# A gated cross-attention layer: new prologue with fp32 row-tiled weight folds, maxima by PE transpose, and double-buffered scores and x

## The chip, the cores and the metric

The kernel runs on one core of one Trainium2 chip. The metric is device time in microseconds (us); the time given is the median over runs. Engines: TensorE (PE), VectorE (DVE), ScalarE (ACT), GpSimd (POOL), and SyncE (SP), which here only issues DMA.

## The reference

```
h   = x + tanh(g_xattn) * (attention(layernorm(x), ctx) @ Wo + bo)
out = h + tanh(g_ffn)   * (layernorm(h) @ W[idx] + b[idx])
attention: q = ln(x) @ Wq, k = ctx @ Wk, v = ctx @ Wv, 16 heads of 64,
           softmax(q k^T / 8) v
idx = argmax(log_softmax(logits) + gumbel(u))       (one of 8 matrices)
```

x is (4, 2048, 512), ctx (4, 77, 384), Wq (512, 1024), Wk and Wv (384, 1024), Wo (1024, 512), W (8, 512, 512), all fp32.

## The kernel before

There are only 77 keys a batch, so the kernel folds the weights once. Prologue: for each batch A = Wq k^T (512 x 16*77) and VW = v Wo (16*77 x 512). Loop: 64 tiles of 128 rows of x, batch by batch in turn, each with scores = ln(x) A, softmax, out = P VW, layer norm and one matrix of the feed-forward.

fp32 precision is kept with fp16 matmuls: an operand is held as high and low fp16 halves and a product is three matmuls (`split_products`, L1014 to 1019). The halves need a power of two as scale, from the largest absolute value over the whole matrix: VectorE takes maxima along the row (`part`, `half`), GpSimd's `partition_all_reduce` (`share`, L453) the maximum over partitions, `power_of_two_scale` (L723) makes the scale.

For the folds (`fold`, L1058) the values and keys are laid out as block diagonals of head pairs (`v_diag`, `k_diag`), so that one 128-row matmul serves two heads: per pair and 128 columns of weights ("a unit") six matmuls of 308 columns. There are 4 slots of 8 units for the values and as many for the keys. ScalarE writes a unit's high half (L619, L643), VectorE the low half (`low`, L290; called at L827 and L841). The folded values are written transposed into `slots`, and 16 DMA transposes (L361, four a slot, on SyncE's queue) bring them into `vw`. `a_split` (the folded keys) lies over the slots, so the key fold waits for transposes (L640, L838).

Before the loop, SyncE then loads the biases and waits for all transposes. The loop is a software pipeline: step n of PE does scores(n), attention(n-1), ffn(n-2) (L1155). VectorE does the softmax of tile n (`maxima`, `shift`, `softmax`, `probs_low`), the layer norm of x tile n+1 (`x_moments` to `x_low`) and the rest of n-1 to n-3. SyncE transposes x (L334), probabilities (L415 to 422) and the second layer norm (L390) by DMA. Scores have three PSUM banks, and the scores of tile n wait for `shifted` of tile n-1 (L1103); x transposed has one buffer (L332). GpSimd computes reciprocal square roots and residual sums. In step (0, 0) VectorE also takes the maxima of the feed-forward matrix, and GpSimd its `share(WF)` (L533); its halves are written in the first steps (L678, L868).

## Time and profile before

| | us |
|---|---|
| median of 3 runs (1121.66 to 1122.82) | 1122.08 |
| the profiled execution: span from first to last instruction | 1116.9 |
| PE busy | 1067.9 (96%) |
| VectorE busy | 964.6 (86%) |
| ScalarE busy | 361.4 (32%) |
| GpSimd busy | 301.4 (27%) |

The span is that of one profiled execution; the times of runs are taken without a profile and include what lies around the span. The mean granted TensorE clock is 0.983 of full. In the rows, a block of a timeline is merged from neighbouring instructions, its name is that of the first, and "xN" counts them. "big", "vw_arena", "banks" are the names of the memory areas; `banks` is PSUM. Lines of helpers (L290 `low`, L1018 `split_products`) stand for all their callers.

### The profile page before, as it was taken

Reading aid. Unit: us, or ns where it says so; the run is one execution under the profiler, and the core shown is the slowest. Engines: PE = TensorE matmul, PEld = TensorE weight load, DVE = VectorE, ACT = ScalarE, POOL = GpSimd, SP = SyncE. Lnnn points to the kernel's source line nnn. Section 1 sums busy time; section 2 is a strip of 40 time slices with the busy share of each in tenths; the row PEclk is TensorE's granted clock in tenths of the full one; section 3 lists DMA queues with packets and bytes.
Section 4 is the critical chain, followed back from the end, with each engine's and each line's share of the span. In section 5 each row is a group of like instructions: output and inputs, shape, how many; then the busy total and the mean of one; then the engine's idle time right before and its main releaser. Section 6 shows DMA issues by size and latency. Waiting matters only on the chain.

```text
span 1116.9 us, 16454 instructions
## 1 busy us (share of the span) xinstructions
PE 1067.9 (96%) x5452; PEld 546.1 (49%) x5452; DVE 964.6 (86%) x1423; ACT 361.4 (32%) x562; POOL 301.4 (27%) x416
## 2 busy tenths in 40 slices
PE   7687879999999999999999999999999999999997
PEld 5455534444454444454544445544445554444542
DVE  6676869999888899888899988889988888998884
ACT  3586432233232223223223323222332322232331
POOL 4361222122222222222222222222222222222221
PEclk9889889999999999999999999999999999999999
DMA  9069625545545544554554554554455455455543
GB/s 327 10 111 200 153 56 113 109 105 121 114 108 116 122 101 111 122 107 109 122 112 104 117 117 108 113 122 104 107 122 111 108 119 114 105 114 115 112 98 76
DMA packets 365720, 129.49 MB, mean 116 GB/s; under 512 B 345039, under 2 KB 345347, under 8 KB 365699
## 3 DMA queue, kind: packets, MB, share of 16 engines
q1 hardware_dynamic: 365635, 129.22, 53.1%
q8 instruction: 12, 0.20, 0.1%
q14 instruction: 9, 0.07, 0.0%
q0 software_dynamic: 64, 0.00, 0.0%
HBM read 26.43 MB, written 16.78 MB: 39 GB/s over the span
## 4 chain that ended last, share of the span: by engine, by line
PE 83%; DVE 6%; ACT 3%; DMA 2%; issue 2%; SPq 2%; POOL 1%; POOLq 0%; DVEq 0%; ACTq 0%
PE banks L1018 81%; PE banks L1137 2%; DVE big L290 2%; SPq L361 2%; DMA big<-big 1%; ACT big L619 1%; DVE big L768 1%; DVE stats L745 1%; DMA xT_area<-big 1%; POOL vw_arena L465 0%; DMA vw_arena<-big 0%; DVE big L892 0%; ACT vw_arena L562 0%; DMA big<-in_ctx 0%; DVE stats L901 0%
## 5 line engine op out<-in xcount | busy, mean ns | idle before, releaser
L1018 PE MATMUL banks<-big,xT_area 128*128 128x462 f16 (+1 forms) x2316 | 418.1, 339 | 11.9 <-DMA xT_area<-big 11.9
L1018 PE MATMUL banks<-vw_arena,big 128*128 128x512 f16 (+1 forms) x1920 | 414.1, 373 | 14.1 <-DVE big L290 8.9
L1018 PEld LDWEIGHTS banks<-big,xT_area 128*128 128x128 f16 x2316 | 226.2, 98 | 204.2 <-DMA xT_area<-big 13.6
L1018 PEld LDWEIGHTS banks<-vw_arena,big 128*128 128x128 f16 (+1 forms) x1920 | 188.3, 99 | 219.3 <-issue 8.7
L1018 PE MATMUL banks<-big 128*128 128x512 f16 (+1 forms) x948 | 203.4, 367 | 10.3 <-DVE big L290 7.2
L524 POOL TENSOR_TENSOR stats<-stats,cst 128x1 f32<-128x1 f32 x64 | 12.3, 192 | 658.2 <-DVE stats L948 658.2
L290 DVE SCALAR_TENSOR_TENSOR big<-big 128x512 f16<-128x512 f32 (+1 forms) x194 | 180.9, 933 | 3.5 <-ACT big L655 1.4
L886 DVE TENSOR_REDUCE stats<-banks 128x6 f32<-128x462 f32 (+1 forms) x192 | 111.7, 582 | 79.0 <-PE banks L1018 78.9
L1018 PEld LDWEIGHTS banks<-big 128*128 128x128 f16 (+1 forms) x948 | 93.3, 99 | 110.5 <-issue 12.5
L700 ACT ACTIVATE big<-big 128x1232 f16<-128x1232 f32 (+1 forms) x66 | 79.2, 1199 | 207.5 <-DVE big L905 207.3
L655 ACT ACTIVATE big<-big 128x512 f16<-128x512 f32 x64 | 40.3, 630 | 326.5 <-DVE big L966 326.5
L686 ACT ACTIVATE big<-big,cst 128x462 f32<-128x462 f32 (+1 forms) x192 | 120.6, 628 | 59.2 <-DVE big L892 59.2
L892 DVE TENSOR_TENSOR big<-banks,stats 128x462 f32<-128x462 f32 (+1 forms) x192 | 111.7, 582 | 2.3
L768 DVE TENSOR_SCALAR big<-big,stats 128x512 f32<-128x512 f32 x64 | 97.8, 1527 | 8.5 <-POOL stats L447 8.5
L905 DVE TENSOR_TENSOR big<-big,cst 128x1232 f32<-128x1232 f32 (+1 forms) x66 | 92.6, 1403 | 2.3
L901 DVE TENSOR_REDUCE stats<-big 128x16 f32<-128x1232 f32 (+1 forms) x66 | 92.2, 1396 | 1.3
L502 POOL TENSOR_TENSOR big<-big 128x512 f32<-128x512 f32 x64 | 83.1, 1300 | 0.1
L537 POOL TENSOR_TENSOR big<-big 128x512 f32<-128x512 f32 x64 | 81.4, 1273 | 3.5 <-DVE big L966 3.5
L571 ACT ACTIVATE big<-big 128x512 f16<-128x512 f32 x64 | 40.3, 630 | 106.4 <-DVE big L768 106.4
L290 DVE SCALAR_TENSOR_TENSOR big<-banks,big 128x616 f32 (+2 forms) x72 | 48.8, 724 | 16.9 <-ACT big L643 11.0
L923 DVE SCALAR_TENSOR_TENSOR big<-banks,cst,big 128x512 f32<-128x512 f32 x64 | 47.7, 746 | 5.2 <-PE banks L1018 5.2
L932 DVE SCALAR_TENSOR_TENSOR big<-banks,cst,big 128x512 f32<-128x512 f32 x64 | 47.7, 745 | 4.6 <-PE banks L1137 4.5
(84 smaller groups left out, 544.9 us busy)
## 6 DMA issues: line engine op xcount, KB each, us to landing
big<-in_x SPq DMA_DIRECT2D x65, 256.0 KB, 2.7
out<-big SPq DMA_DIRECT2D x64, 256.0 KB, 2.2
big<-big SPq DMA_TRANSPOSE x133, 3.2
vw_arena<-in_L_xattn_Wq SPq DMA_DIRECT2D x2, 1024.0 KB, 12.8
vw_arena<-in_L_xattn_Wo SPq DMA_DIRECT2D x2, 1024.0 KB, 16.8
big<-in_L_xattn_Wv SPq DMA_DIRECT2D x2, 768.0 KB, 8.2
big<-in_L_xattn_Wk SPq DMA_DIRECT2D x2, 768.0 KB, 14.8
xT_area<-big SPq DMA_TRANSPOSE x65, 3.1
```

The costliest lines, as they stand in the source:

```text
L290: return nc.vector.scalar_tensor_tensor(out=lo, in0=value, scalar=scale, in1=hi, op0=ALU.mult, op1=ALU.subtract)
L502: nc.gpsimd.tensor_tensor(res[:, b1, :], xin[:, b1 % 2, :], bias[:, 0, :], ALU.add).then_inc(res_ready, 1)
L537: nc.gpsimd.tensor_tensor(res[:, b2, :], res[:, b2, :], bias[:, 1, :], ALU.add).then_inc(x2b_ready, 1)
L686: nc.scalar.activation(probs[:, cols], probs[:, cols], ACT.Exp, scale=exp_scale).then_inc(exp_done, 1)
L700: nc.scalar.activation(ps[:, h0 * J:h1 * J], probs[:, h0 * J:h1 * J], ACT.Copy, scale=2.0 ** PROB_BITS).then_inc(p_hi, 1)
L768: nc.vector.tensor_scalar(xn, xin[:, b1 % 2, :], mv1[:, 0:1], rstd1, ALU.subtract, ALU.mult).then_inc(xn_ready, 1)
L886: nc.vector.reduce_max(mx[:, h0:h1], by_head(s_ps[:, k, 0:(h1 - h0) * J]), AX.X).then_inc(mx_ready, 1)
L892: nc.vector.tensor_tensor(by_head(probs[:, h0 * J:h1 * J]), by_head(s_ps[:, k, 0:(h1 - h0) * J]), mx[:, h0:h1].unsqueeze(2).to_broadcast([ ...
L901: nc.vector.reduce_sum(sums[:, h0:h1], values, AX.X).then_inc(sum_ready, 1)
L905: nc.vector.tensor_tensor(values, values, factors.unsqueeze(2).to_broadcast([P, h1 - h0, J]), ALU.mult).then_inc(p_ready, 1)
L923: nc.vector.scalar_tensor_tensor(out=outb[:, b3 % 2, :], in0=f_ps, scalar=f_scale, in1=res[:, b3, :], op0=ALU.mult, op1=ALU.add).then_inc( ...
L1018: mm = nc.tensor.matmul(ps, lhs(l), rhs(r), start=first and n == 0, stop=last and n == 2)
```

## The change

- Folds: no block diagonals and no fp16 halves of the operands. A unit is two fp32 matmuls of 64 rows each (`unit`), head e = 0 on partitions 0 to 63 into one bank, e = 1 on partitions 64 to 127 into the next. Only the result is split into halves. vT (and wqT when it is copied out of PSUM) is multiplied by one product of scales. All 64 units are written out instead of partly looped. PE's value fold has three bank pairs, the key fold four.
- Key matmuls stand between the units of the value fold (`key_piece`). The queries' transposes come at its end.
- Maxima over partitions: a PE transpose of the column of maxima, spread over 128 columns, and a VectorE maximum along the row (`spread`, `power_of_two`). GpSimd's `partition_all_reduce` is gone everywhere.
- Load order: Wv, Wo, Wk, W[idx], Wq; x tiles 0 and 1 after the value fold, from ScalarE's queue. The feed-forward matrix is scaled and split in the prologue by GpSimd and ScalarE. Key maxima, Wq maxima and the x preparation of tiles 0 and 1 stand between the units on VectorE.
- Memory: raw weights and ctx lie where the transposed values (`vw`) go; `a_split` lies over the slots and the raw feed-forward matrix; the key fold of quarter k waits for the transposes of slot k. SyncE's order is slots 0 to 2, x tile 0, biases, slot 3, x tile 1.
- Loop: scores alternate between banks 0 to 2 and 5 to 7 and wait for `shifted` of tile n-2; x transposed has two buffers. The first scores wait for the whole key fold. Step (0, 0) no longer holds x and matrix work.

The core of the diff:

```diff
+        fold_area = sb("fold_area", [P, KT * SLOT_WORDS])
+        a_split = fold_area[:, 0:A_WORDS].bitcast(F16).rearrange("p (k s b n) -> p k s b n", s=2, k=KT, b=B)
+        slots = fold_area[:, :].bitcast(F16).rearrange("p (t b n) -> p t b n", t=KT, b=B)
...
+        vw_area = sb("vw_area", [P, KT * SLOT_WORDS])
+        vw = vw_area[:, :].bitcast(F16).rearrange("p (t b c n) -> p t b c n", t=KT, b=B, n=P)
...
-        s_ps = banks[:, 0:3, :]
+        s_ps = [banks[:, 0:3, :], banks[:, 5:8, :]]
...
+        V_BANKS = [0, 4, 2]
+        A_BANKS = [6, 2, 0, 4]
...
+        def pair_banks(first):
+            return banks[:, first:first + 2, 0:BJ].rearrange("p e (b j) -> p e b j", b=B)
...
+        def pair_of_heads(cols):
+            return cols.rearrange("p b (e j) -> p e b j", e=2)
...
-                if n == 0:
-                    sp.dma_start(xin[:, 0, :], x[0, 0:P, :]).then_inc(x_first, 16)
...
-                sp.dma_start(wq_raw[:, rows, :], wq.rearrange("(k p) n -> p k n", p=P)[:, rows, :]).then_inc(wq_loaded[n], 16)
...
             sp.wait_ge(idx_ready, 1)
...
             sp.dma_start(wf_raw, ffn_w[bass.ds(op, 1), :, :].rearrange("o (k p) n -> p (o k) n", p=P)).then_inc(wf_loaded, 16)
...
-                if positive(q1, b1, 1):
-                    due(s_done, nth(q1, b1, len(BANKS)))
-                sp.dma_start_transpose(xT.rearrange("p s k n -> p (s k) n"),
+                if positive(q1, b1, 2):
+                    due(s_done, nth(q1, b1, len(BANKS)) - len(BANKS))
+                sp.dma_start_transpose(xT[:, b1 % 2].rearrange("p s k n -> p (s k) n"),
...
+            for t in range(KT - 1):
+                turn_values(t)
+            turn_x(0, 0)
+            sp.wait_ge(vwT_done, 2 * UNITS)
             sp.dma_start(bias[:, 0, :], bo.rearrange("(a n) -> a n", a=1).to_broadcast([P, D])).then_inc(bias_loaded, 16)
...
+            turn_values(KT - 1)
+            turn_x(0, 1)
...
-            def share(k):
...
-                pool.wait_ge(amax_ready, k + 1)
-                nc.gpsimd.partition_all_reduce(amax_all[:, k:k + 1], amax[:, k:k + 1], P,
-                                               bass.bass_isa.ReduceOp.max).then_inc(amax_shared, 1)
...
+            pool.wait_ge(scale_f_ready, 1)
+            nc.gpsimd.tensor_tensor(wf_flat, wf_flat, scale_f.to_broadcast([P, KT * D]), ALU.mult).then_inc(wf_scaled, 1)
...
+            act.wait_ge(scale_v_ready, 1)
...
+            nc.scalar.activation(vT[:, 5:HP, :], vT[:, 5:HP, :], ACT.Copy, scale=scale_v).then_inc(v_scaled_end, 1)
...
+                act.wait_ge(vwT_done, 2 * (u + 1))
+                nc.scalar.copy(pair_of_heads(slots[:, t, :, h * PW:(h + 1) * PW]), pair_banks(V_BANKS[u % 3])).then_inc(vwT_hi, 1)
...
+                for h in range(HP):
+                    value_high(t, h)
+                act.wait_ge(vwT_hi, (t + 1) * HP)
+                nc.scalar.copy(slots[:, t, :, LOW + BODY:LOW + BODY + TAIL], slots[:, t, :, BODY:HJ]).then_inc(vwT_tail, 1)
...
+            for r in range(2):
+                act.dma_start(xin[:, r, :], x[r, 0:P, :]).then_inc(x_loaded[r], 16)
...
+            for h in range(0, HP, 2):
+                act.wait_ge(wqT_done, h + 1)
+                nc.scalar.activation(wqT[:, h, :], banks[:, WQ_BANKS[h], :], ACT.Copy, scale=scale_q).then_inc(wqT_even, 1)
...
+                    v = k * HP + h
+                    act.wait_ge(a_done, 2 * (v + 1))
+                    nc.scalar.copy(pair_of_heads(a_split[:, k, 0, :, h * PW:(h + 1) * PW]), pair_banks(A_BANKS[v % 4])).then_inc(a_hi, 1)
+                    if v == 5:
+                        x_high(0, 0)
+                    if v == 22:
+                        x_high(0, 1)
...
+            def power_of_two(m, bank):
...
+                dve.wait_ge(amax_spread[m], 1)
+                nc.vector.reduce_max(top[:, m:m + 1], banks[:, bank, 0:P], AX.X).then_inc(pow_step[m], 1)
+                dve.wait_ge(pow_step[m], 1)
+                nc.vector.tensor_scalar(pow2[:, m:m + 1].bitcast(U32), top[:, m:m + 1].bitcast(U32), 0x7F800000, None,
+                                        ALU.bitwise_and).then_inc(pow_step[m], 1)
+                dve.wait_ge(pow_step[m], 2)
+                nc.vector.reciprocal(rcp[:, m:m + 1], pow2[:, m:m + 1]).then_inc(pow_step[m], 1)
...
+            dve.wait_ge(floor_set, 1)
+            value_part(0)
...
+                dve.wait_ge(wo_loaded[n], 16)
+                part(WO, n, wo_raw[:, n * HP // 2:(n + 1) * HP // 2, :])
+            largest(WO)
+            value_part(1)
+            value_part(2)
+            value_part(3)
+            largest(VV)
+            power_of_two(WO, 4)
+            power_of_two(VV, 0)
...
+            nc.vector.scalar_tensor_tensor(out=scale_v, in0=rcp[:, VV:VV + 1], scalar=2.0 ** FOLD_BITS, in1=rcp[:, WO:WO + 1],
...
+            dve.wait_ge(scale_v_ready, 1)
+            for h0, h1 in ((0, 2), (2, 5)):
+                nc.vector.tensor_scalar(vT[:, h0:h1, :], vT[:, h0:h1, :], scale_v, None, ALU.mult).then_inc(v_scaled, 1)
...
+            dve.wait_ge(wf_loaded, 16)
+            part(WF, 0, wf_raw)
+            largest(WF)
...
+            def value_low(t, h):
...
+                first = V_BANKS[u % 3]
+                dve.wait_ge(vwT_hi, u + 1)
+                if h < HP - 1:
...
+                    nc.vector.tensor_tensor(pair_of_heads(slots[:, t, :, LOW + h * PW:LOW + (h + 1) * PW]), pair_banks(first),
+                                            pair_of_heads(slots[:, t, :, cols]), ALU.subtract).then_inc(vwT_lo, 1)
+                else:
+                    for e, start, stop, beyond in LAST_LOWS:
+                        key = (HEADS - 2 + e) * J
+                        nc.vector.tensor_tensor(slots[:, t, :, key + beyond + start:key + beyond + stop], one_bank(first, e, start, stop),
+                                                slots[:, t, :, key + start:key + stop], ALU.subtract).then_inc(vwT_lo, 1)
...
+                    value_low(t, h)
+                    if (t, h) == (0, 1):
+                        power_of_two(WF, 7)
+                        dve.wait_ge(pow_step[WF], 3)
+                        nc.vector.tensor_scalar(scale_f, rcp[:, WF:WF + 1], 2.0 ** WF_BITS, None, ALU.mult).then_inc(scale_f_ready, 1)
+                    if (t, h) == (0, 3):
+                        key_part(0)
+                    if (t, h) == (KT - 1, 3):
+                        power_of_two(KK, 6)
+                        power_of_two(WQ, 7)
...
+                        nc.vector.scalar_tensor_tensor(out=scale_q, in0=rcp[:, KK:KK + 1], scalar=2.0 ** FOLD_BITS, in1=rcp[:, WQ:WQ + 1],
...
+                    if t == 1 and h in (2, 5):
+                        n = h // 3
+                        dve.wait_ge(wq_loaded[n], 16)
+                        part(WQ, n, wq_raw[:, n * KT // 2:(n + 1) * KT // 2, :])
+                if t < KT - 1:
+                    key_part(t + 1)
+                if t == 1:
+                    largest(WQ)
+                if t == 2:
+                    largest(KK)
...
+                    dve.wait_ge(a_hi, v + 1)
+                    nc.vector.tensor_tensor(pair_of_heads(a_split[:, k, 1, :, cols]), pair_banks(A_BANKS[v % 4]),
+                                            pair_of_heads(a_split[:, k, 0, :, cols]), ALU.subtract).then_inc(a_lo, 1)
+                    if v == 1:
+                        x_moments(0, 0)
+                    if v == 2:
+                        dve.wait_ge(x_stats, 1)
+                        x_variance()
+                    if v == 4:
+                        x_normalized(0, 0)
+                    if v == 6:
+                        x_low(0, 0)
+                    if v == 8:
+                        x_moments(0, 1)
+                    if v == 9:
+                        dve.wait_ge(x_stats, 2)
+                        x_variance()
+                    if v == 12:
+                        x_normalized(0, 1)
+                    if v == 24:
+                        x_low(0, 1)
...
+            def spread(m, bank):
...
+                pe.wait_ge(amax_ready[m], 1)
+                nc.tensor.transpose(banks[:, bank, 0:P], amax[:, m:m + 1].to_broadcast([P, P]), ident[:, :]).then_inc(amax_spread[m], 1)
...
+            def key_piece(h, k):
...
+                if k == 0 and h == 2:
+                    pe.wait_ge(v_copied, HP // 2)
+                if k == 0 and h >= 4:
+                    pe.wait_ge(k_copied, h // 2)
+                mm = nc.tensor.matmul(banks[:, k_bank(h), 0:BJ], wk_raw[:, k, h * P:(h + 1) * P], ctxT[:, k, :],
+                                      start=k == 0, stop=k == CT - 1)
...
+            pe.wait_ge(v_copied, 3)
+            spread(WO, 4)
...
+            def unit(first, weights, data, t, h, done):
...
+                for e in range(2):
+                    rows = slice(DH * e, DH * e + DH)
+                    nc.tensor.matmul(banks[:, first + e, 0:BJ], weights[rows, h, t * P:(t + 1) * P], data[rows, h, :],
+                                     start=True, stop=True).then_inc(done, 1)
...
+            for t in range(KT):
                 for h in range(HP):
+                    u = t * HP + h
+                    if u >= 3:
+                        pe.wait_ge(vwT_lo, lows_after(u - 3))
+                    if u == 0:
+                        pe.wait_ge(v_scaled, 1)
+                        pe.wait_ge(pow_step[VV], 1)
+                    if u == 1:
+                        pe.wait_ge(pow_step[WO], 1)
+                    if u == 2:
+                        pe.wait_ge(v_scaled, 2)
+                        pe.wait_ge(k_copied, 1)
+                    if u == 5:
+                        pe.wait_ge(v_scaled_end, 1)
+                    unit(V_BANKS[u % 3], wo_raw, vT, t, h, vwT_done)
+                    if u == 0:
+                        pe.wait_ge(v_copied, HP // 2)
+                        spread(WF, 7)
+                    if u == 1:
+                        pe.wait_ge(pow_step[WF], 1)
+                    if t < KT - 1 and h % 4:
+                        key_piece(2 + 2 * t + h // 4, h % 4 - 1)
+                    if t == KT - 1:
+                        if h == 3:
+                            pe.wait_ge(k_copied, HP // 2)
+                            spread(KK, 6)
+                            spread(WQ, 7)
+                        if h == 5:
+                            pe.wait_ge(pow_step[KK], 1)
+                            for n in range(2):
+                                pe.wait_ge(wq_loaded[n], 16)
+                            query_turned(0)
+                        if h == 6:
+                            pe.wait_ge(pow_step[WQ], 1)
+                            query_turned(1)
+            for h in range(2, HP):
+                pe.wait_ge(vwT_lo, lows_after(UNITS - 4 + h // 2))
+                query_turned(h)
...
+            for k in range(KT):
+                for h in range(HP):
+                    v = k * HP + h
+                    if v < 4:
+                        pe.wait_ge(wqT_even, v + 1)
+                        pe.wait_ge(wqT_odd, v + 1)
...
                 for n, (h0, h1) in enumerate(BANKS):
-                    if positive(q, b, 1):
-                        pe.wait_ge(shifted, nth(q, b, len(BANKS)) + n + 1 - len(BANKS))
+                    if positive(q, b, 2):
+                        pe.wait_ge(shifted, nth(q, b, len(BANKS)) + n + 1 - 2 * len(BANKS))
                     else:
...
-                        pe.wait_ge(a_lo, (KT - 1) * HP + max(-(-h1 // 2), HP // 2 + n // 2 + 1))
+                        pe.wait_ge(a_lo, UNITS)
                     for k in range(KT):
-                        mm = split_products(s_ps[:, n, 0:(h1 - h0) * J], lambda s: xT[:, s, k, :],
+                        mm = split_products(s_ps[b % 2][:, n, 0:(h1 - h0) * J], lambda s: xT[:, b % 2, s, k, :],
                                             lambda s: a_split[:, k, s, b, h0 * J:h1 * J], k == 0, k == KT - 1)
                     mm.then_inc(s_done, 1)
```

## Rows read from the trace of the kernel before

**Rows 1.** The page: busy time of each engine, and granted clock in 40 slices.

```profile
PE 1067.9 (96%) x5452; PEld 546.1 (49%) x5452; DVE 964.6 (86%) x1423; ACT 361.4 (32%) x562; POOL 301.4 (27%) x416
...
PEclk9889889999999999999999999999999999999999
```

**Rows 2.** Busy time by stretch: length, busy us (instructions) by engine, PEclk, DMA share, GB/s.

```profile
140.00:160.00 20.00, 12.36 (x47) 5.12 (x45) 11.18 (x21) 5.62 (x7) 2.02 (x3) 0.74 0.25 53
...
400.00:1000.00 600.00, 600.00 (x3062) 298.46 (x3061) 541.53 (x796) 176.19 (x278) 159.19 (x240) 1.00 0.52 113
```

**Rows 3.** PE's timeline in the steady loop: start, duration, what ran, count.

```profile
603.04 5.99 PE L1018 MATMUL banks<-vw_arena,big 128*128 128x512 f16 x27
...
609.30 2.75 PE L1018 MATMUL banks<-big 128*128 128x512 f16 x12
...
611.89 6.42 PE L1018 MATMUL banks<-big,xT_area 128*128 128x462 f16 x36
...
618.15 5.99 PE L1018 MATMUL banks<-vw_arena,big 128*128 128x512 f16 x27
```

**Rows 4.** PE's timeline of the first four score blocks; brackets hold idle time before.

```profile
122.41 6.42 PE L1018 MATMUL banks<-big,xT_area 128*128 128x462 f16 x36
...
132.03 8.11 PE L1018 MATMUL banks<-big,xT_area 128*128 128x462 f16 x36 [3.21 <-DMA xT_area<-big]
...
154.05 9.34 PE L1018 MATMUL banks<-big,xT_area 128*128 128x462 f16 x36 [7.64 <-DMA xT_area<-big]
...
172.10 6.43 PE L1018 MATMUL banks<-big,xT_area 128*128 128x462 f16 x36
```

**Rows 5.** Chain of waits to 230 us: start, duration, step.

```profile
103.50 5.20 DMA vw_arena<-big
...
139.46 6.90 issue
```

**Rows 6.** SyncE's queue: issue of the transposes of folded values and first probabilities.

```profile
67.15 45.92 SPq L361 DMA_TRANSPOSE vw_arena<-big  x14
...
134.85 2.58 SPq L415 DMA_TRANSPOSE big<-big  x2
...
138.84 1.19 SPq L422 DMA_TRANSPOSE big<-big  x1
...
174.78 3.06 SPq L422 DMA_TRANSPOSE big<-big  x1
```

**Rows 7.** Timeline of single steps before the folds.

```profile
12.92 10.19 PEld L1034 LDWEIGHTS banks<-vw_arena,big 128*128 128x128 f32 x39 [0.18 <-issue]
...
23.64 0.67 ACT L578 COPY big<-banks 128x616 f32<-128x616 f32 x1 [2.44 <-PE banks L1034]
...
24.37 0.15 DVE L728 TENSOR_SCALAR cst<-cst 128x1 uint32<-128x1 uint32 x1
```

**Rows 8.** Groups by line and shape, first 200 us: busy us, mean ns | idle.

```profile
L643 ACT ACTIVATE big<-banks 128x616 f16<-128x616 f32 x32 | 21.2, 685 | 12.6 <-DMA vw_arena<-big 7.4 <-PE banks L1018 3.5
...
L1034 PE MATMUL banks<-vw_arena,big 128*128 128x308 f32 x48 | 14.9, 478 | 1.5 <-DMA big<-in_L_xattn_Wv 1.5
...
L1034 PEld LDWEIGHTS banks<-vw_arena,big 128*128 128x128 f32 x48 | 10.4, 220 | 5.7 <-issue 3.1
...
L745 DVE TENSOR_REDUCE stats<-vw_arena 128x1 f32<-128x2048 f32 x4 | 9.0, 2272 | 0.0
...
L738 DVE TENSOR_REDUCE cst<-big 128x1 f32<-128x616 f32 x4 | 3.1, 785 | 0.0
...
L678 ACT ACTIVATE big<-wf_area,cst 128x2048 f16<-128x2048 f32 x1 | 2.0, 2002 | 1.9 <-DVE cst L733 1.9
```

**Rows 9.** VectorE's densest stretch of fold subtractions.

```profile
90.25 12.03 DVE L290 SCALAR_TENSOR_TENSOR big<-banks,big 128x616 f16<-128x616 f32 x16 [1.58 <-ACT big L643]
```

**Rows 10.** VectorE: normalizing an x tile without company, and a softmax sum.

```profile
125.99 0.55 DVE L768 TENSOR_SCALAR big<-big,stats 128x512 f32<-128x512 f32 x1 [0.47 <-POOL stats L447]
...
168.75 1.44 DVE L901 TENSOR_REDUCE stats<-big 128x16 f32<-128x1232 f32 x1
```

579 lines of the change are left out of this document (191 added, 388 removed).

## The prediction

> **What bounds the kernel now.** I read the page first. PE is busy 96% of the span, and its granted clock is nine tenths or more except in slices 2, 3, 5 and 6 of 40 [rows 1]. So there are two regimes. In the stretch from 400 to 1000 us PE is busy 600.00 of 600.00 us while VectorE is busy 541.53 [rows 2]: nobody makes PE wait, and only less matmul work could help. One tile is the distance between two attention blocks, 618.15 - 603.04 = 15.11 us: attention 6.26 (to 609.30, its two tail matmuls included), feed-forward 2.59, scores 6.26 in step, 6.42 to the last end [rows 3]. The change leaves columns and count of these matmuls alone; double-buffered scores remove a wait that has no idle time here. I give the loop 0, tail included, and expect all of the effect before tile 3.
>
> That prologue reads so. The first scores begin at 122.41. They should be followed without a gap; instead the second begin at 132.03 after 3.21 us idle and last 8.11, the third at 154.05 after 7.64 us idle and last 9.34, the fourth begin at 172.10 [rows 4]. The granted clock of the stretch from 140 to 160 is 0.74, a mixture of 2.4 and 1.2 GHz [rows 2]: after such waits a block runs partly at the lower level. From 172.10 to 611.89 are 439.8 us, and 29 tiles of 15.11 are 438.2: another 1.6 us of stalls. So the loop "starts" at an effective 173.7.
>
> The chain of waits holds the two causes. 6.90 us of "issue" at 139.46 follow a cross-partition maximum on GpSimd (there is the like ahead of the one for the keys); they hold up the third tile's square root, and so make the gap before 154.05. And at 103.50 it waits 5.20 us for a transposed slot to land [rows 5]. That belongs to the 16 DMA transposes of the folded values. SyncE issues the first at 67.15 [rows 6]; the twelfth is the one issued at 103.50, so the pace is (103.50 - 67.15)/11 = 3.30 us each. The fold of the keys may overwrite a slot only when it has been transposed.
>
> **The change step by step.** I carry one time for each engine.
>
> Start of the value fold. The value matmuls stay and end near 23.4; the copy at 23.64 ends at 24.3 [rows 7]. VectorE has by then taken both maxima of Wo, which now loads ahead of Wk and Wq. Left are one maximum of 616 (0.79 [rows 8]), six tiny steps at 0.18 (the distance of the 0.15 us steps of [rows 7]), a PE transpose with its wait, and scaling 616 and 924 elements of vT (0.62 and 0.98, taken from the 0.79 for 616): about 28.7. Then the maximum of the feed-forward matrix, 2048 elements, 2.27 [rows 8]: 31.2. Its PE transpose stands between unit 0 and unit 1 in PE's queue, so everybody waits for this: the fold runs from 31.2.
>
> Cost of a fold unit (one head pair, 616 results a partition). ScalarE 0.69 [rows 8]. VectorE: 16 in 12.03 us, 0.75 each [rows 9]; tensor_tensor in place of scalar_tensor_tensor reads the same two streams and I give it no gain (bounds: -0.1 and +0.15). PE: the old unit is six fp16 matmuls. The new one is two fp32 matmuls over 64 rows, each two instructions. The nearest rows are full-height fp32 matmuls of the same width: 39 weight loads in 10.19 us, 0.26 per instruction [rows 7]. Four in series are 1.04 us; two pairs side by side in the two halves of the array 0.52. With nothing of the weight loads hidden (0.22 each [rows 8]) a unit is 1.9. No 64-row matmul is in this trace. I take 0.52 as likeliest, with VectorE then the pace. The Trainium skill, "TensorE: Matmul & The Clock Gate", section on packing small matmuls, says that matmuls in different row groups run concurrently, starting some 4 ns apart; by it the unit is the 0.52, and otherwise the 1.04. No run here shows it yet.
>
> Value fold on VectorE. A slot is 7 x 0.76 + 1.1 for the last pair's four pieces = 6.4. Slot 0 adds 1.1 for restarting behind the transpose, 0.8 for a scale, 0.8 for a key maximum: ready at 40.4. ScalarE then has a tail copy, a key copy and the matrix's fp16 half (0.46, 0.67, 2.00 [rows 8]) ahead of slot 1's first copy, so VectorE resumes at 43.6. Slot 1 adds two Wq maxima of 2.27: 54.5. Slot 2: 61.9. Slot 3 adds two scales, 1.7, and the key parts in between 1.9: 71.0. Half of wqT, 4 x 0.70, makes 73.9. PE needs 32 x 0.52 + 18 key matmuls x 0.52 = 26 us in these 40 and is hidden; in series it needs 43 and adds about 3.
>
> Transposes. They start at 40.5, not 67.15. Slot 0 to 53.7, slot 1 54.6 to 67.8, slot 2 to 81.0 (four at 3.30 each). Now the x tile's transpose stands ahead of slot 3 in SyncE's queue, and needs x_low(0, 0), which VectorE reaches after seven key units: 73.9 + 7 x 0.76 + 2.1 for x (0.68 and 0.18 moments, 0.55 [rows 10], 0.69) = 81.3. They meet almost exactly. Transpose 1.24 and two bias loads 0.92 make 83.7; the fourth transpose of slot 3 is issued at 93.6 and landed (5.2) at 98.8.
>
> Key fold. VectorE alone would be through three quarters at 73.9 + 24 x 0.76 + 4.2 = 96.3, so ScalarE waits for slot 3 until 98.8. Copy 0.69, eight subtractions 6.2 and x_low(0, 1) 0.6: 106.2. All of it is needed by the first scores, so they begin at 106.2 in place of 122.41. That is less than the 26.7 us by which the transposes start earlier, because VectorE becomes the limit too.
>
> Start of the loop. Both x tiles are ready, so scores(1) follow scores(0), to 12.8 us after their start. Softmax(0): its last shift ends 7.4 after the start (bank 2 is done at 6.4), and by the old spacing from 131.3 the first transposes are issued 3.6 later and both landed by 15.4 [rows 6]: PE idles 2.6. Attention to 22.0. x(2) on VectorE follows the 5.1 us of softmax(0) and takes 6.6 with tile 1's maxima between, then 3.1 for the transpose: 22.2. Scores(2) to 28.6. Softmax(1) (1.44 [rows 10], 0.25, 1.44, attention sum 1.44, low half 1.44) puts the transpose at 25.2, landed 30.1: 1.5 idle. Attention 6.6, feed-forward 2.7: scores(3) 39.4 after the first, and I add 1.0 for a block at the lower clock. Before, this stretch took 173.7 - 122.4 = 51.3. The gain of 10.9 is the custom maximum that is gone and the second x buffer.
>
> GpSimd's new work (two passes over 2048 elements, some 8 us) is due only before slot 3 at 62 and is covered; uncovered it would cost a few us there. Loop: 0.
>
> Sum: 106.2 + 40.4 = 146.6 against 173.7, 27.1 less. The profiled span 1116.9 becomes 1089.8; the median 1122.08 stands 5.2 above the span, all that lies around it, so 1095.0.
>
> **What the page on tiling adds.** In the trace PE changes between kinds of matmul with no visible gap [rows 3]. The Trainium skill, "TensorEngine Tiling (Array Packing)", tiling modes, says that changing the tiling mode drains the array. The 18 key matmuls, full height, stand between half-height units; that would be up to 36 drains. This speaks against the interleaving and is rival B.
>
> **Rivals.** A: the halves don't overlap, 1.04 a unit. Slot 0 is ready at 43.5, the key fold starts near 76.5 and needs 32 x 1.04 = 33.3 plus 1.5: first scores at 111.3, time 1100. For it: nothing in the trace overlaps two fp32 matmuls. B: in series and 36 mode changes at about 0.27 each (a 128-column transpose from start to end, the shortest matmul here, as the size of an empty pipe): 9.7 us on a value fold that is then PE's, first scores near 119.5, time 1108. If only the drains are real, 26 + 10 = 36 stays below VectorE's 40. C, the other sign: PE per unit above 1.4 us, because weight loads in front of 64-row matmuls are exposed or the clock stays at the lower level through the folds. First scores are about 44 + 64c; equal to before at c = 1.40. At the exposed 1.9 they begin at 166, time 1155. Against it: the fp32 value matmuls hide their loads at full clock [rows 7]. D: the prologue gains, but the start of the loop doesn't, because the softmax chain of tiles 0 and 1 and the x preparation queue behind one another on VectorE: 10.9 lost, 1106.
>
> **How the numbers follow.** Forecast 1095 with 0.50 (own range 1088 to 1100), A 0.22, B 0.08, C 0.08, D 0.09, the rest something that eats nearly everything. Range 1086 to 1110: it takes in A, B and D, and 3 us for a VectorE subtraction cheaper than assumed. Faster by over 0.2% (2.2 us, what a measurement can tell) 0.89, within 0.2% 0.03, slower 0.08.
>
> **What would show it.** Unit pace: row of PE's fold matmuls, 0.76 a unit with PE half idle (forecast), 1.04 with PE full (A), more (C). First value transposed at 40 or 41; slot 3's first transpose at 83 to 84; first scores at 106; fourth scores 40 us later; no idle block over 3 us after the first scores; 15.11 per tile unchanged. Wrong would be: a tile period that moves, VectorE's fp32-and-fp16 subtraction over two banks above 0.8 us, or a transpose pace other than 3.3.

## The result, and the profile after

| | before | after |
|---|---|---|
| median of 4 runs each on one occasion, us | 1122.35 (1121.66 to 1122.82) | 1103.03 (1102.12 to 1105.92) |
| profiled span, us | 1116.9 | 1100.8 |
| PE busy, us | 1067.9 | 1060.8 |
| mean granted TensorE clock | 0.983 | 0.988 |

The ratio is 0.9838, with a 95% interval of 0.9823 to 0.9854: 19.3 us faster, where 27.1 were forecast. The time, 1103.0, lies inside the range of 1086 to 1110 and outside the narrower one of 1088 to 1100 that the forecast had for itself.

The page of the profile still has PE at 96%, and the low clock is confined to the first slices, as in [rows 1]:

```profile
PE 1060.8 (96%) x5329; PEld 526.3 (48%) x5329; DVE 948.3 (86%) x1417; ACT 344.6 (31%) x545; POOL 266.7 (24%) x402
...
PEclk9799899999999999999999999999999999999999
```

Busy time by stretch, columns as in [rows 2]. The loop is what it was, PE busy 600.00 of 600.00 us. The stretch from 27 to 45 us is the beginning of the value fold: PE busy 13.87 of 18 us at a mean clock of 0.62.

```profile
27.00:45.00 18.00, 13.87 (x41) 5.73 (x41) 8.79 (x15) 5.48 (x9) 3.60 (x1) 0.62 0.05 18
...
400.00:1000.00 600.00, 600.00 (x3062) 298.18 (x3061) 541.30 (x797) 176.27 (x278) 158.84 (x240) 1.00 0.50 113
```

PE's timeline from the key fold to the steady loop, beside [rows 3, 4]:

```profile
95.28 7.85 PE L961 MATMUL banks<-late 64*128 64x308 f32 x44 [0.37 <-DVE fold_area L744]
110.33 4.60 PE L961 MATMUL banks<-late 64*128 64x308 f32 x16 [7.20 <-DVE fold_area L744]
116.66 12.67 PE L906 MATMUL banks<-fold_area,early 128*128 128x462 f16 x72 [1.74 <-DVE fold_area L744]
132.05 7.49 PE L906 MATMUL banks<-vw_area,late 128*128 128x512 f16 x27 [2.72 <-issue]
...
139.81 6.42 PE L906 MATMUL banks<-fold_area,early 128*128 128x462 f16 x36
147.82 6.00 PE L906 MATMUL banks<-vw_area,late 128*128 128x512 f16 x27 [1.60 <-DMA late<-late]
...
156.69 6.42 PE L906 MATMUL banks<-fold_area,early 128*128 128x462 f16 x36
...
602.20 5.99 PE L906 MATMUL banks<-vw_area,late 128*128 128x512 f16 x27
...
617.31 5.99 PE L906 MATMUL banks<-vw_area,late 128*128 128x512 f16 x27
```

The first 72 matmuls are scores(0) and scores(1) in one piece. Read backwards: the tile period is 617.31 - 602.20 = 15.11 us, unchanged. The fourth scores begin at 156.69, 40.03 after the first; forecast 40.4. The two idle pieces before the attentions are 2.72 and 1.60; forecast 2.6 and 1.5. So the loop and its start are as forecast, and the miss sits in one number: the first scores begin at 116.66, not 106.2.

SyncE's queue, beside [rows 6], says where that comes from (its durations are those of issuing; a transpose lands later):

```profile
47.57 40.73 SPq L327 DMA_TRANSPOSE vw_area<-fold_area  x12
89.27 1.23 SPq L305 DMA_TRANSPOSE early<-early  x1
...
91.86 15.03 SPq L327 DMA_TRANSPOSE vw_area<-fold_area  x4
```

The first transpose is issued at 47.57 where I had 40.5. The chain of waits, beside [rows 5], comes to the x transpose (89.27) from VectorE's low half of x tile 0, `x_low(0, 0)`, and not from the twelfth slot transpose, whose issue is over at 88.30. It ends this part with the last transpose, issued at 103.74, under way, `103.74 4.93 DMA`; it lands at 108.67:

```profile
88.57 0.61 DVE early L271
...
100.52 3.17 SPq L327
103.74 4.93 DMA vw_area<-fold_area
109.47 0.81 DVE fold_area L744
```

The 10.46 us of the miss, piece by piece, forecast against trace:

| piece | forecast | trace | miss |
|---|---|---|---|
| first value transpose issued | 40.5 | 47.57 | 7.07 |
| from there to the x transpose, behind 12 slot transposes and `x_low(0, 0)` | 40.8 | 41.70 | 0.90 |
| x transpose and biases | 2.4 | 2.59 | 0.19 |
| slot 3's first issue to its last landing | 15.1 | 16.81 | 1.71 |
| landing to first scores | 7.4 | 7.99 | 0.59 |

Seven of ten are slot 0. PE's timeline there (a unit is "x4" at L961, a third of a key product "x2" at L938, the spread of a maximum "x1" at L928):

```profile
26.81 0.79 PE L961 MATMUL banks<-early 64*128 64x308 f32 x4
29.90 0.44 PE L928 MATMUL banks<-ident,red 128*128 128x128 f32 x1 [2.30 <-DVE red L626]
30.27 1.40 PE L961 MATMUL banks<-early 64*128 64x308 f32 x4
33.51 1.40 PE L938 MATMUL banks<-vw_area 128*128 128x308 f32 x2 [1.84 <-DVE red L631]
34.83 1.40 PE L961 MATMUL banks<-early 64*128 64x308 f32 x4
36.16 1.39 PE L938 MATMUL banks<-vw_area 128*128 128x308 f32 x2
37.49 1.40 PE L961 MATMUL banks<-early 64*128 64x308 f32 x4
...
43.42 0.79 PE L961 MATMUL banks<-early 64*128 64x308 f32 x4
44.14 0.79 PE L938 MATMUL banks<-vw_area 128*128 128x308 f32 x2
44.86 0.79 PE L961 MATMUL banks<-early 64*128 64x308 f32 x4
...
46.29 1.31 PE L961 MATMUL banks<-early 64*128 64x308 f32 x8
```

Unit 0 takes 0.79 us from start to end and unit 1 1.40: between them PE idled 2.30 us for VectorE's maximum of the feed-forward matrix, and 1.84 more for its first reduction. From there a unit with its key matmul takes some 2.65 us (34.83 to 37.49); from 43.42 on the pair takes 1.44. The granted clock from 30 to 43 us was 0.50, the lower of the two levels. So slot 0 is late by the clock and by the second wait.

The groups by line and shape from 24 to 110 us, beside [rows 8]:

```profile
L698 DVE TENSOR_TENSOR fold_area<-banks,fold_area 128x616 f16<-128x616 f32 x28 | 21.4, 794 | 12.6 <-ACT fold_area L515 12.6
...
L744 DVE TENSOR_TENSOR fold_area<-banks,fold_area 128x616 f16<-128x616 f32 x25 | 18.5, 787 | 8.2 <-ACT fold_area L543 8.2
```

VectorE's subtraction is 0.79 from start to end as before, and 11 of them one after the other take 7.85 us, 0.71 each (0.75 in [rows 9]), which is also PE's pace for the 44 instructions at 95.28. tensor_tensor brings 0.04 us at most; it was priced at nothing.

### The profile page after: what moved, and what is told of

Same layout as the page of the kernel before. It is cut to its first block, busy times and chain, and to the rows that moved or that the text cites. A ratio compares the mean times of both kernels' runs of the same rounds, so it can differ in the third digit from the quotient of the medians.

```text
span 1100.8 us, 15901 instructions
## 1 busy us (share of the span) xinstructions
PE 1060.8 (96%) x5329; PEld 526.3 (48%) x5329; DVE 948.3 (86%) x1417; ACT 344.6 (31%) x545; POOL 266.7 (24%) x402
## 4 chain that ended last, share of the span: by engine, by line
PE 88%; DVE 5%; DMA 3%; ACT 1%; SPq 1%; issue 1%; POOL 0%; ACTq 0%; DVEq 0%
PE banks L906 81%; PE banks L1052 2%; DMA late<-late 2%; PE banks L961 2%; PE banks L921 1%; SPq L327 1%; PE banks L938 1%; DVE red L621 1%; DVE fold_area L698 1%; DVE late L271 1%; DMA vw_area<-in_L_xattn_Wv 1%; DVE fold_area L744 1%; DMA vw_area<-fold_area 0%; ACT fold_area L515 0%; DVE stats L806 0%
## 5 line engine op out<-in xcount | busy, mean ns | idle before, releaser
L906 PE MATMUL banks<-fold_area,early 128*128 128x462 f16 (+1 forms) x2304 | 410.6, 336 | 1.7 <-DVE fold_area L744 1.7
L906 PE MATMUL banks<-vw_area,late 128*128 128x512 f16 x1701 | 378.9, 380 | 5.3 <-issue 2.7
L906 PEld LDWEIGHTS banks<-fold_area,early 128*128 128x128 f16 x2304 | 223.9, 97 | 189.3 <-issue 2.4
L906 PEld LDWEIGHTS banks<-vw_area,late 128*128 128x128 f16 x1701 | 166.5, 98 | 197.4 <-issue 6.2
L906 PE MATMUL banks<-wf_split,late 128*128 128x512 f16 x756 | 174.8, 381 | 2.8 <-POOL stats L458 2.8
L583 ACT ACTIVATE late<-late,cst 128x462 f32<-128x462 f32 (+1 forms) x192 | 120.7, 628 | 59.2 <-DVE late L797 59.2
L271 DVE SCALAR_TENSOR_TENSOR late<-late 128x512 f16<-128x512 f32 (+2 forms) x130 | 136.6, 1052 | 1.4 <-ACT late L558 1.4
L797 DVE TENSOR_TENSOR late<-banks,stats 128x462 f32<-128x462 f32 (+1 forms) x192 | 111.6, 581 | 2.3
L650 DVE TENSOR_SCALAR early<-early,stats 128x512 f32<-128x512 f32 x64 | 94.2, 1471 | 0.0
L420 POOL TENSOR_TENSOR early<-early 128x512 f32<-128x512 f32 x64 | 83.3, 1301 | 0.1
L467 POOL TENSOR_TENSOR early<-early 128x512 f32<-128x512 f32 x64 | 81.1, 1267 | 3.5 <-DVE late L864 3.5
## 6 DMA issues: line engine op xcount, KB each, us to landing
vw_area<-in_L_xattn_Wk SPq DMA_DIRECT2D x2, 768.0 KB, 15.1
```

What stands on the lines that cost most here:

```text
L271: return nc.vector.scalar_tensor_tensor(out=lo, in0=value, scalar=scale, in1=hi, op0=ALU.mult, op1=ALU.subtract)
L420: nc.gpsimd.tensor_tensor(res[:, b1, :], xin[:, b1 % 2, :], bias[:, 0, :], ALU.add).then_inc(res_ready, 1)
L467: nc.gpsimd.tensor_tensor(res[:, b2, :], res[:, b2, :], bias[:, 1, :], ALU.add).then_inc(x2b_ready, 1)
L583: nc.scalar.activation(probs[:, cols], probs[:, cols], ACT.Exp, scale=exp_scale).then_inc(exp_done, 1)
L650: nc.vector.tensor_scalar(xn, xin[:, b1 % 2, :], mv1[:, 0:1], rstd1, ALU.subtract, ALU.mult).then_inc(xn_ready, 1)
L797: nc.vector.tensor_tensor(by_head(probs[:, h0 * J:h1 * J]), by_head(s_ps[b % 2][:, k, 0:(h1 - h0) * J]), mx[:, h0:h1].unsqueeze(2).to_broa ...
```

## The experiments

The first number is the median in us, the range of its runs stands in parentheses, and the ratio is to the kernel before on the same chip, with its interval. Except for the two kernels made from the one before, each is the changed kernel with the edit shown.

**The theory**: the waits on the feed-forward matrix's maximum idle PE at the start of the value fold, the clock falls, slot 0 comes 7 us late, and the chain of 16 transposes hands this on one for one. **The rivals**: the half-height fp32 matmuls, or their changes of shape, hold the pace down by themselves; or the transposes aren't what the first scores wait for.

### The wait moved (theory against the shapes)

```diff
                     if u == 0:
...
+                        pe.wait_ge(v_copied, HP // 2)
...
-                    if u == 0:
-                        pe.wait_ge(v_copied, HP // 2)
+                    if u == 2:
                         spread(WF, 7)
-                    if u == 1:
+                    if u == 4:
                         pe.wait_ge(pow_step[WF], 1)
```

> The changed kernel with one move: PE does value units 0, 1 and 2 before the transpose of the feed-forward matrix's maxima, instead of unit 0 alone. Theory (a PE wait drops the clock): the idle of 2.3 us after unit 0 and 1.8 us after unit 1 are what holds PE at 1.2 GHz from 30.3 to 43 us, so slot 0 of the folded values is ready at 47.5 instead of 40.4. Without the idle the units stay at 0.30 us per four weight loads, slot 0 is ready at 40 to 41, the first value transpose is issued at 41, and the first scores come 5 to 7 us earlier: about 1097. Rival (64-row fp32 matmuls hold the clock low by themselves): PE is still at the lower level from 30 to 43, slot 0 at 46 or later, time 1101 to 1103.

Measured 1097.90 (1094.45 to 1099.07), ratio 0.9796 (0.9778 to 0.9815). The stretch of the value fold's start, columns as in [rows 2]:

```profile
27.00:45.00 18.00, 16.68 (x78) 7.55 (x77) 15.29 (x25) 12.52 (x19) 7.75 (x3) 1.00 0.32 67
```

PE's timeline, with the moved spread and the first scores:

```profile
30.43 0.32 PE L928 MATMUL banks<-ident,red 128*128 128x128 f32 x1 [0.21 <-DVE red L626]
...
107.79 12.67 PE L906 MATMUL banks<-fold_area,early 128*128 128x462 f16 x72 [1.73 <-DVE fold_area L744]
```

SyncE's queue:

```profile
38.95 41.24 SPq L327 DMA_TRANSPOSE vw_area<-fold_area  x12
```

The clock is full with the same shapes in the same alternation, so these do not bring it down by themselves. The transposes begin 8.6 us earlier than in the changed kernel and the first scores 8.9: handed on one for one. The move takes away the idle time and the lower clock together, and no run has one without the other. The rows give the shares: the seven blocks from 33.51 to 43.42 in the changed kernel, 9.9 us, take 5.8 at this kernel's pace, and unit 1 takes 0.6 less, so about 4.8 us are the clock (an estimate from the two timelines); the two waits are 2.30 and 1.84.

The profiled execution was the fastest of its four, and its span is 8.2 shorter; the median is 5.1 lower. Run again:

> The version with the late feed-forward spread once more, beside the other two on one chip. If the chain of 16 transposes gates the first scores, it is 2.5 to 4 us slower than the version with all three: 1094 to 1096 where that one has 1091.

Measured 1097.38 (1092.63 to 1098.93), ratio 0.9776 (0.9757 to 0.9795), 6.4 us above the version with all three edits (below), where 2.5 to 4 were expected. PE's timeline of this run's profiled execution, the same program:

```profile
110.18 14.20 PE L906 MATMUL banks<-fold_area,early 128*128 128x462 f16 x72 [1.73 <-DVE fold_area L744]
```

One program's two profiled executions differ by 2.4 us in when the first scores begin and by 1.5 in how long these last, and its runs spread over 6 us. So much can lie between a trace and a median here. In this second execution the transposes begin at 40.67 and the gains are 6.9 and 6.5 us: still one for one, but smaller, and nearer to the gain of the medians (5.1 and 5.7).

### The key matmuls grouped (what the changes of shape cost)

```diff
-                    if t < KT - 1 and h % 4:
-                        key_piece(2 + 2 * t + h // 4, h % 4 - 1)
+                    if t < KT - 1 and h % 4 == 3:
+                        for k in range(CT):
+                            key_piece(2 + 2 * t + h // 4, k)
```

> The changed kernel with the three matmuls of a key head behind one value unit (h = 3 and 7) instead of one behind each of three units. Theory (each change between 64-row and 128-row matmuls costs PE about 0.20 us at full clock and 0.30 at the lower): a slot has 4 changes instead of 12, so 1.6 us less PE time a slot (2.4 in slot 0), slot 0 ready at about 45, first scores 2 us earlier, time 1100 to 1101. Rival (changes cost nothing on the path, VectorE sets the pace): slot 0 at 47.5 as before, 1103.

Measured 1102.31 (1100.63 to 1105.78), ratio 0.9827 (0.9805 to 0.985): no different from the changed kernel, and not the 1100 to 1101 expected. SyncE's queue:

```profile
43.98 43.13 SPq L327 DMA_TRANSPOSE vw_area<-fold_area  x12
89.00 1.23 SPq L305 DMA_TRANSPOSE early<-early  x1
```

Slot 0 is 3.6 us earlier, where eight changes fewer at 0.30 us had made me expect 2.4. The rest is the clock, which with the same two waits came back sooner: 0.81 over the stretch in which the changed kernel had 0.62, and three units in a row at full pace from 38.84 on, where that kernel was at the lower one until 42.5. Part of this is spread between executions: the single-buffered kernel below, whose value fold is that of the changed kernel, had 0.72 and its first transpose at 46.95, so the gain in slot 0 is 3.0 to 3.6.

```profile
27.00:45.00 18.00, 13.14 (x57) 6.94 (x57) 11.61 (x21) 8.35 (x13) 3.60 (x1) 0.81 0.04 14
```

```profile
38.84 1.82 PE L961 MATMUL banks<-early 64*128 64x308 f32 x12
```

So the alternation of shapes does not by itself bring the clock down, but with it the clock stayed down longer than without (few executions; no run tests this alone).

The x transpose stands at 89.00 as in the changed kernel (89.27). It waits for VectorE's `x_low(0, 0)`, and slot 3 queues behind it. By the end of the value fold only 1.2 us of the 3.6 are left (76.48 against 77.68), and there VectorE waits 0.62 us more for the load of x tile 0, which ScalarE issues behind the value fold and which lands 6.4 us later. So an earlier slot 0 alone is not handed on: this edit opens one gate, and the others lie close behind it. With the late wait and the grouping together:

> The changed kernel with both the late feed-forward spread and the key matmuls in threes. Theory (with PE at full clock VectorE sets the pace of the value fold, so 8 changes of array shape fewer a slot, at 0.20 us each, are covered): within 1.5 us of the late spread alone, 1096.5 to 1099. Rival (changes of shape still on the path): slot 0 ready 1.6 us earlier and 1095 or less.

1093.45 (1091.95 to 1095.59), ratio 0.9758 (0.9735 to 0.978), better than the 1096.5 to 1099 expected, as the rival had it, but not by the rival's mechanism: the transposes begin at 38.81 and the first scores at 108.69, no earlier than with the late wait alone. In its profile all of the loop's start runs at full clock (attention(0) 5.99 us, not 7.45 as with the late wait alone). The span is 2.0 us shorter than in the first profile of the late wait alone, the median 4.4 less. Whether the gain is this clock after the fold or spread between executions stays open.

### Both halves on the same rows (do they run side by side?)

```diff
-                    rows = slice(DH * e, DH * e + DH)
+                    rows = slice(0, DH)
```

> The changed kernel with both matmuls of every fold unit on the data rows 0 to 63 (the second head's fold is wrong). Theory (the two matmuls of a unit run side by side because they sit in different rows of the array): here they run one after the other, a unit in the key fold takes 1.03 us instead of 0.71, the first scores come 8 to 15 us later, 1112 to 1118. Rival (the pace of 0.52 us for four instructions has nothing to do with the rows): time unchanged at 1103.

One run: 1164.29, span 1162.5. The expectation was right in direction and four times or more too small in size (8 to 15 us expected, 61 measured). PE's timeline of it, then busy time by stretch:

```profile
44.91 4.47 PE L961 MATMUL banks<-early 64*128 64x308 f32 x8
...
135.01 29.29 PE L961 MATMUL banks<-late 64*128 64x308 f32 x112
```

```profile
45.00:80.00 35.00, 35.00 (x60) 17.25 (x60) 14.33 (x19) 10.29 (x14) 4.21 (x2) 0.50 0.41 75
80.00:110.00 30.00, 30.00 (x52) 14.34 (x50) 8.43 (x15) 7.47 (x12) 0.00 (x0) 0.50 0.47 87
135.00:165.00 30.00, 29.30 (x113) 20.86 (x112) 21.94 (x32) 18.23 (x29) 4.80 (x7) 1.00 0.64 114
```

At full clock (1.00 from 135 us on) a unit in series is 29.29/28 = 1.05 us, as rival A had it (1.04), against 0.52 side by side (from one unit to the next inside the "x8" of 1.31 us at 46.29 after). But from 45 to 110 us, nearly the whole value fold, the clock stayed at 1.2 GHz, with PE busy 65.00 of 65.00 us, and a unit was 2.05 and more. That is rival C, of which I had said that the trace was against it; it did not come true with the halves side by side. This kernel still has the two waits in front (1.78 and 1.80 us). Whether they, or the work in series by itself, kept the clock down is open: no run has the series without the waits.

### Only the custom maximum replaced, in the kernel before

```diff
-                nc.gpsimd.partition_all_reduce(amax_all[:, k:k + 1], amax[:, k:k + 1], P,
-                                               bass.bass_isa.ReduceOp.max).then_inc(amax_shared, 1)
+                nc.gpsimd.tensor_tensor(amax_all[:, k:k + 1], amax[:, k:k + 1], amax[:, k:k + 1], ALU.add).then_inc(amax_shared, 1)
```

> The kernel before with GpSimd's maximum over partitions replaced by a plain GpSimd addition on the same column (each partition keeps its own maximum as scale, which makes the folds wrong). Theory (the custom instruction costs some 6 us of loading before each run after ordinary work): the maximum for the keys no longer waits 5.7 us, the first value transpose is issued near 62 instead of 67, and the third tile's scores no longer wait 7.6 us, together 8 to 13 us: 1109 to 1114. Rival (the transposes and the VectorE queue hide it): within 3 us of 1122.

Measured 1103.17 (1102.21 to 1105.34), ratio 0.9846 (0.9824 to 0.9867): 18.5 us, half as much again as the 13 that I expected at most, and nearly as much as the whole change. Its SyncE queue, then PE's timeline:

```profile
57.53 46.01 SPq L361 DMA_TRANSPOSE vw_arena<-big  x14
```

```profile
113.06 6.42 PE L1017 MATMUL banks<-big,xT_area 128*128 128x462 f16 x36
...
137.38 6.43 PE L1017 MATMUL banks<-big,xT_area 128*128 128x462 f16 x36 [0.32 <-DMA xT_area<-big]
...
155.36 6.43 PE L1017 MATMUL banks<-big,xT_area 128*128 128x462 f16 x36 [0.93 <-DMA xT_area<-big]
```

Beside [rows 4, 6]: transposes 9.6 us earlier (67.15 to 57.53), first scores 9.35 earlier (122.41 to 113.06), and the gap before the third scores 0.32 where it was 7.64, so that first to fourth scores take 42.30 instead of 49.69. Removing only the feed-forward matrix's custom maximum separates the two places:

```diff
+                if k == WF:
+                    nc.gpsimd.tensor_tensor(amax_all[:, k:k + 1], amax[:, k:k + 1], amax[:, k:k + 1], ALU.add).then_inc(amax_shared, 1)
+                    return
```

> The kernel before with only the last of GpSimd's maxima over partitions (the one for the feed-forward matrix, in the loop's first step) replaced by a plain addition (this matrix's scale then differs by partition and its product is wrong). Theory (two separate stalls): the first value transpose stays at 67, the third tile's scores no longer wait 7.6 us, and the time falls by 6 to 8 us to 1114. The rest of the 18.5 us that all replacements gave then belongs to the maximum for the keys and the GpSimd work behind it. Rival (one stall feeds the other): no gain, or all of it, at the second alone.

1112.26 (1111.43 to 1113.97), ratio 0.9918 (0.9898 to 0.9938): 8.6 of the 18.5, all after the first scores (these at 123.15, and 43.1 from there to the fourth), a little more than the 6 to 8 expected. The other half lies before the value fold, where the chain of waits of the kernel before has the like of the 6.90 of [rows 5]:

```profile
51.57 5.66 issue
57.23 0.39 POOL cst L456
```

5.66 us are less than the 9.6 by which the transposes come earlier. A second such piece seems to stand behind the first three maxima: GpSimd's next ordinary operation starts at 41.28 in the kernel before, 7.12 us after the last of them, and at 35.75 with ordinary operations in their place. The profile puts this wait down to ScalarE, so that part is argued and not shown.

### Scores and x single-buffered again, in the changed kernel

```diff
-                    if positive(q, b, 2):
-                        pe.wait_ge(shifted, nth(q, b, len(BANKS)) + n + 1 - 2 * len(BANKS))
+                    if positive(q, b, 1):
+                        pe.wait_ge(shifted, nth(q, b, len(BANKS)) + n + 1 - len(BANKS))
```

(and the like for the x transpose)

> The changed kernel with the waits of single buffering put back: x of tile n+1 is transposed only after the scores of tile n, and scores wait for the shifts of tile n-1 (two buffers stay in memory). Theory (double buffering gives only the start of the loop): the second scores begin 3 us after the first end, since their x is transposed then; part of it is covered by the wait for the first softmax. Time 1 to 3 us longer than the changed kernel, 1104 to 1106; the period of 15.11 us a tile is unchanged. Rival (it also helps the steady loop): a period above 15.11 and over 5 us.

1105.98 (1102.62 to 1107.93), ratio 0.9854 (0.9831 to 0.9878), inside the 1104 to 1106 expected. In PE's timeline scores(1) wait for x again, and the fourth scores begin 43.49 after the first (116.15 to 159.64), 3.5 more than after:

```profile
127.39 9.22 PE L906 MATMUL banks<-fold_area,early 128*128 128x462 f16 x36 [3.23 <-DMA early<-early]
...
159.64 6.42 PE L906 MATMUL banks<-fold_area,early 128*128 128x462 f16 x36
```

The tile period stays 15.11. By the trace the double buffers are worth 3.5 us, once; the medians differ by 3.0, but the two ratios' intervals overlap, so the runs alone do not show it.

### The queue in another order

Slot 3 ahead of the x transpose and the biases, on top of the late wait; tile 1's x halves move behind the key fold's units 30 and 31, so that VectorE and ScalarE don't stand in its way:

```diff
-            for t in range(KT - 1):
+            for t in range(KT):
                 turn_values(t)
             turn_x(0, 0)
...
-            turn_values(KT - 1)
```

> The version with the late feed-forward spread (first scores at 107.8, median 1097.9), with SyncE's order changed: all four slots are transposed before x tile 0 and the biases; the second x tile's halves move to key units 30 and 31. Theory (the landing of the 16th value transpose gates the last quarter of the key fold): slot 3's transposes start right behind slot 2's, 3.1 us earlier, and the first scores come 2.5 to 3.1 us earlier, at about 105: 1095. Rival (VectorE's queue or PE's pace sets the end of the key fold): first scores move by less than 1 us, 1097 to 1098.

1091.30 (1088.89 to 1093.03), ratio 0.9726 (0.9708 to 0.9745). Expected were a time of 1095 and first scores at 105. First scores at 103.52 against 107.79 with the late wait alone, though they ran partly at 1.2 GHz (14.36 us). Of these 4.3 us 0.9 is an earlier first transpose (38.07 against 38.95). With the late wait alone 3.06 us lie between the twelfth transpose and slot 3 (80.19 to 83.25): the x transpose and the biases were on the path in full. All three edits together:

> Late feed-forward spread, key matmuls in threes and all slots transposed before the first x tile, together. Theory (the transposes are one chain from slot 0 to slot 3, and nothing else gates the key fold): slot 0 starts at 38.5, the chain of 16 takes 55 to 56 us, first scores at 103 to 104 as with the late spread and the order alone; the grouping adds nothing: within 1 us of that version, 1090 to 1092. Rival (x_low hid a gain of the grouping): 1.5 us less or more.

1090.94 (1088.84 to 1091.11), ratio 0.9726 (0.9713 to 0.9739): the best version, by the medians 30 us faster than before and 12 faster than the change, but, as expected, no further than order and late wait alone. Its SyncE queue, then PE's timeline:

```profile
39.34 54.36 SPq L327 DMA_TRANSPOSE vw_area<-fold_area  x16
```

```profile
102.33 14.35 PE L905 MATMUL banks<-fold_area,early 128*128 128x462 f16 x72 [2.13 <-DVE fold_area L743]
```

And without the late wait, the other two edits kept:

> The same without the late spread: PE again waits for the feed-forward matrix's maximum between units 0 and 1. Theory (the wait and the lower clock after it cost by themselves what slot 0 is late, and the chain of transposes hands it on one for one): slot 0's first transpose near 44 as with the grouping alone, first scores 5 us later than in the version with all three, 1095 to 1097. Rival (the order alone buys the gain): within 2 us of the version with all three.

1099.05 (1095.4 to 1099.44), ratio 0.9792 (0.9774 to 0.9811): 8.1 us slower than all three, where 1095 to 1097 was expected; first scores at 109.09 against 102.33, 6.8 later, of which 5.3 are there at the first transpose (44.67 against 39.34) and 1.4 come in the chain of 16 itself (55.78 against 54.36 us). So the late wait is worth 7 to 8 us once the x transpose is out of the way. In the changed kernel it was 5.1 and 5.7 by the medians and 6.5 and 8.9 by the traces; the two cannot be told apart.

## Why the prediction was right, and where it was not

**Luck in the number.** The profiled span was forecast at 1089.8 and is 1100.8, 11.0 us off; the median is only 8.0 off. The forecast had put 5.2 us around the span, the difference between a median and the span of one execution. In the four runs after, each time is 1.8 or 1.9 us above its own span. So 3 us of the miss are hidden by that constant: the gain is 16.1 us by the two spans and 19.3 by the medians. And the range of 1086 to 1110 had been made wide for A, B and D, none of which came true; its width is why it holds a miss of another cause.

**Right: what bounds, and what the loop does.** 0 for the loop (15.11 a tile in both). The fourth scores 40.03 after the first against 40.4, with both idle pieces within 0.12 us (block lengths differ: attention(0) took 7.49 us at the lower clock, for which the forecast had 1.0 in hand); that part of the gain, 49.69 to 40.03 from first to fourth scores, was also credited rightly: 7.4 us of it come with the custom maximum alone, and 3.5 go when the buffers are single (the two overlap and do not add up to it). Rival D is out.

**Right: the halves run side by side** (0.52 a unit; rival A out, and 1.05 is its price).

The Trainium skill, "TensorE: Matmul & The Clock Gate", section on packing small matmuls, has matmuls in different row groups run concurrently; the trace agrees, 0.52 us for the four instructions of a unit against 1.05 on the same rows.

**Wrong: the step "Start of the value fold".** I had seen that the spread stands between units 0 and 1, and took it as a delay of the start that costs 1.1 us for restarting. What it costs most is the clock: slot 0's units ran at 1.2 GHz until 43 us, in pairs of some 2.65 us instead of 1.44. Slot 0 was in hand at 47.5, not 40.4. By the estimate above about 4.8 of the 7.1 us are the clock; the rest is the second wait of 1.84, of which the forecast had only the 1.1, and PE's pairs of 1.44, which at full clock too are longer than the 0.76 that I had as the pace. The late wait shows the two waits and the clock together (transposes from 38.95 and 40.67 in two executions, about my 40.5), and leaving it out of the best version costs 8.1 us. The sentence that PE "needs 26 us in these 40 and is hidden" holds as a sum over the fold, not for its first slot, nor, by the chain of waits, for its third, which lies on PE from 59.34 to 67.88: there PE is the one that all wait for, and [rows 4] had shown what a wait does to the next block. I had used that for one block after the first scores and not here.

**Changes of shape, rival B.** At full clock two units follow each other 0.52 apart, a unit and a key matmul 0.72: 0.20 us for a change, near the 0.27 I had bounded it by. I gave it nothing in the forecast because VectorE would cover it; over the first and the third slot it was not covered. The 3.0 to 3.6 us of the grouped kernel are fewer changes (2.4 at 0.30 each) and an earlier return of the clock. Rival B as I wrote it (in series and with changes, 1108) was not what happened.

The Trainium skill, "TensorEngine Tiling (Array Packing)", key properties of the tiling modes, says that switching the mode drains the array; the trace agrees, with 0.20 us a change at 2.4 GHz.

**Mis-sized: the transposes of slot 3.** From the first issue to the fourth are 11.88 us (91.86 to 103.74), 3.96 each, priced at 3.30: 2.0 us more. The way from the last issue to landing was 4.93, 0.3 less than the 5.2 priced. The first twelve took 3.39 each (40.73/12), but the x transpose waited longer, for `x_low(0, 0)`, by 0.97 us.

**Right, and not carried far enough: the new gate.** Before, the last quarter of the key fold needed the twelfth slot transpose; now it needs the sixteenth, with the x transpose and the biases ahead of slot 3. The forecast had this order in its sum (that is why 26.7 us of earlier transposes gave only 16.2), but gave as the reason only that VectorE becomes the limit too. Up to the x transpose that is so (`x_low(0, 0)` came last). From there it is the queue: in ScalarE's timeline after,

```profile
108.69 2.41 ACT L543 CAST fold_area<-banks 128x616 f16<-128x616 f32 x4 [7.25 <-DMA vw_area<-fold_area]
```

ScalarE idles 7.25 us for slot 3, and VectorE and PE with it (7.19 and 7.20). Taking the x transpose out of the queue's way gave 4.3 us of first scores, 3.4 of them behind the first transpose. This also answers why the whole change is no faster than replacing the custom maximum alone: transposes start 10.0 us earlier than in that kernel (47.57 against 57.53) and end behind a later gate, first scores at 116.66 against 113.06; the double buffers and the prepared tile 1 give 2.3 back by the fourth scores, and the last 1.2 lie behind those; I did not trace them.

**Open.** Whether a key fold whose last quarter doesn't lie over slot 3 would bring the first scores forward by four more transposes: not tried. Whether the clock would stay up with the halves in series and no wait in front: not tried either. Why the first 72 score matmuls run 12.67 us in some kernels and 14.3 in others is also open; it changes between executions of one kernel.

## What to carry to other kernels

Price a wait of two microseconds in front of a chain of small matmuls also by the clock it leaves behind (here about 4.8 us for waits of 2.3 and 1.8), and put a late operand's transpose where its data is surely there. When a stage is made faster, look at what the next stage's buffers lie over: the overlay here moved the gate from the twelfth to the sixteenth transfer, and then the queue's order was worth more than the shapes of the matmuls. And price the oddest instruction by itself first: replacing one custom operation gave here nearly all that a new prologue gave.

## What the runs showed of the hardware

- TensorE stayed at 1.2 GHz while it was busy without a gap: from 33.51 to 42.5 us after (units and key matmuls in turn), and from 45 to 110 us in the serial kernel, 65.00 of 65.00 us. With the same shapes as after and no wait of over 0.21 us in front of them it stayed at 2.4 from 27 to 45 us; with the waits and the key matmuls grouped it was back at 38.84. Full-height fp16 blocks recovered within one block (`132.05 7.49`, then 6.42).
- Two fp32 matmuls of 64 rows and 308 columns on the two halves of the array take 0.52 us together, on the same half 1.05. A change between half and full height costs 0.20 us at 2.4 GHz and 0.30 at the lower clock (an estimate: a pair of unit and key matmul is 1.44 and 2.65, the two alone 2 x 0.52 and 2 x 1.02, and the pair has two changes).
- Around the custom maximum on GpSimd the chain of waits has pieces of "issue" of 5.66 and 6.90 us with no work in them; an ordinary operation in its place, five times, took 18.5 us off the kernel.
